# Sixteen small scalings on ScalarE, a second queue for turned inverses, and an earlier residual

## The reference

```python
q, k, v = causal_dwconv(x @ Wq.T), causal_dwconv(x @ Wk.T), causal_dwconv(x @ Wv.T)   # 4 taps and a bias each
g, beta = log_sigmoid(x @ Wg.T), sigmoid(x @ Wb.T)
k = k / clip(norm(k), 1e-12); q = q * 64 ** -0.5
for t in range(T):                 # S: 64x64 per sequence and head
    S = exp(g[t]) * S + beta[t] * (outer(v[t], k[t]) - outer(S k[t], k[t]))
    o[t] = S q[t]
x = layernorm(x + o @ Wo.T)        # then the experts, and layernorm again
```

## Time and profile before

| | |
|---|---|
| median of 3 runs | 1891.66 us (1887.62 to 1893.59) |
| profiled execution | 1890.86 us, span 1888.9 us |
| busy over the span | TensorE 1621.4, VectorE 1302.2, ScalarE 669.4, GpSimd 1068.5 us |
| 203 to 1160 us (957 us) | TensorE 909.0, VectorE 889.8, ScalarE 426.9, GpSimd 557.3 us; granted clock 1.00 |
| 64 to 203 us (139 us) | TensorE 114.3, VectorE 109.3, ScalarE 57.8, GpSimd 65.0 us; granted clock 0.93 |
| 1160 to 1276 us (116 us) | TensorE 89.6, VectorE 63.9, ScalarE 32.3, GpSimd 38.1 us; granted clock 0.92 |
| line 847, 64 operations | 91.3 us, mean 1427 ns |
| line 853, 64 operations | 67.6 us, mean 1056 ns |
| line 851, 64 operations | 132.3 us, mean 2067 ns |

### The profile page before, as it was taken

The page is one execution under the profiler, slowest core; times in us unless marked ns, Lnnn a source line. Parts: engine busy times, 40 slices in busy tenths (PEclk is TensorE's granted clock), DMA queues, the critical chain, the costliest instruction groups (busy, mean ns, idle before and its releaser), DMA issues. The chain is left out here.

```text
span 1888.9 us, 72945 instructions
## 1 busy us (share of the span) xinstructions
PE 1621.4 (86%) x31244; PEld 1239.6 (66%) x31244; DVE 1302.2 (69%) x3029; ACT 669.4 (35%) x1290; POOL 1068.5 (57%) x1261
## 2 busy tenths in 40 slices
PE   7479999999999999999999999776999995798950
PEld 6236666666666666666666666665888885787840
DVE  1388999999999999999899999623555553222214
ACT  1244444444444444444444444211111211233313
POOL 0155565565565565655556556412777776577853
PEclk9799999999999999999999999988999998899985
DMA  6245555555555546555545545425554551699557
GB/s 264 84 83 108 109 110 119 120 111 117 123 107 122 121 102 122 113 109 115 122 109 110 118 111 106 89 53 178 165 172 148 173 149 52 186 252 224 95 93 234
DMA packets 530210, 245.39 MB, mean 130 GB/s; under 512 B 423504, under 2 KB 497872, under 8 KB 528992
## 3 DMA queue, kind: packets, MB, share of 16 engines
q1 hardware_dynamic: 443872, 204.95, 43.5%
q0 software_dynamic: 18432, 18.99, 5.8%
q10 hardware_dynamic: 67584, 16.79, 4.0%
HBM read 169.29 MB, written 71.37 MB: 127 GB/s over the span
## 5 line engine op out<-in xcount | busy, mean ns | idle before, releaser
L373 PE MATMUL delta_p_j<-delta_xt,delta_w 128*128 128x512 f32 x768 | 389.2, 630 | 30.0 <-DMA delta_xt<-in_xt 17.4
L572 DVE SCALAR_TENSOR_TENSOR delta_kq<-delta_hist,cw,delta_kq 128x512 f32<-128x512 f32 x384 | 367.6, 957 | 32.6 <-ACT delta_kq L718 23.6
L711 ACT ACTIVATE delta_hist<-delta_p_j 128x512 f32<-128x512 f32 x192 | 114.9, 599 | 473.2 <-PE delta_p_j L373 464.9
L373 PEld LDWEIGHTS delta_p_j<-delta_xt,delta_w 128*128 128x128 f32 x768 | 132.5, 192 | 145.8 <-issue 112.3
L1220 POOL DMA_INDIRECT slot_tokens<-mix_tokens,mix_slot x192 | 189.9, 989 | 62.4 <-issue 61.8
L860 POOL TENSOR_TENSOR delta_sd<-state,eg_end 128x256 f32<-128x256 f32 x128 | 104.9, 820 | 203.1 <-DVE state L652 203.1
L586 DVE SCALAR_TENSOR_TENSOR delta_yv<-delta_hist,cw,delta_yv 128x512 f32<-128x512 f32 x128 | 166.3, 1299 | 7.5 <-ACT delta_yv L718 5.3
L434 PEld LDWEIGHTS delta_p_i<-delta_kkq,rt 64*64 64x64 f32 x4096 | 130.5, 135 | 59.1 <-issue 44.0
L492 PEld LDWEIGHTS delta_p_c<-delta_r,delta_kkq 64*64 64x64 f32 x2048 | 70.9, 136 | 125.1 <-DVE delta_r L644 71.3
L1343 DVE SCALAR_TENSOR_TENSOR expert_gate<-expert_gate,expert_p_h 88x256 f32<-88x256 f32 x64 | 26.7, 417 | 176.9 <-ACT expert_gate L1363 176.9
L434 PE MATMUL delta_p_i<-delta_kkq,rt 64*64 64x32 f32 (+1 forms) x4096 | 141.6, 213 | 4.5 <-DVE delta_kkq L636 3.8
(11 more groups left out here) (145 smaller groups left out, 3699.5 us busy)
## 6 DMA issues: line engine op xcount, KB each, us to landing
delta_xd<-x_scratch SPq DMA_DIRECT2D x256, 128.0 KB, 4.4
delta_w<-in_wqkv SPq DMA_DIRECT2D x64, 416.0 KB
w<-in_w SPq DMA_DIRECT2D x64, 352.0 KB
delta_eg<-eg_rows SPq DMA_DIRECT2D x128, 130.0 KB
n_scratch<-delta_kkq ACTq DMA_DIRECT2D x128, 128.0 KB
mix_ot<-ot SPq DMA_DIRECT2D x16, 1024.0 KB, 5.7
w<-in_w SPq DMA_DIRECT2D x64, 176.0 KB
ot<-delta_o SPq DMA_DIRECT2D x32, 256.0 KB
```

What stands on the lines that cost most here:

```text
L373: mm = pe.matmul(p_j[:, :], w[e][:, (ch * 3 + n) * 128:(ch * 3 + n) * 128 + 128], xt[m // 8 % 2][:, ch * 512:ch * 512 + 512], start=ch == ...
L572: ve.scalar_tensor_tensor(out, view(hist[e], i * 2 * 518 + tap, (259, 2), (1, 256)), cw[:, column:column + 1], out, ALU.mult, ALU.add).the ...
L711: ac.activation(view(hist[e], n * 518 + 3, (259, 2), (1, 256)), p_j[:, :], ACT.Copy)
```

## The change

- The two scalings move from GpSimd to ScalarE, as 8 activations of 128x64 each with the factor as a per-partition scale. `scale_keys(t-1)` stands at the end of ScalarE's slot, `scale_values(t-2)` in two groups of four, before the exponential and after `turned_r`. GpSimd keeps the power (`roots`), and waits in `factors` and `roots` until the scalings of the macro before are done.
- The turned inverses are stored by ScalarE on its DMA queue, right after it has turned them, under their own semaphore. `load_inverse` waits for them first and issues the two loads of the turned half under a semaphore of their own, then waits for the plain store and issues the other two.
- VectorE's second residual stands behind the first of the three key taps.
- GpSimd does the first decay and the off-diagonal mask before carry in.

```diff
             def load_inverse(m):
-                sp.wait_ge(x_out[group % 2], 32 * (group // 2 + 1))
+                sp.wait_ge(xt_out[group % 2], 16 * (group // 2 + 1))
                 for sh in range(2):
...
+                    sp.dma_start(view(xd[e], 512, (C, 8), (1, C), parts=half(sh)),
...
+                                         [[C, C], [UNIT, 8], [1, C]])).then_inc(xdt_in[e], 16)
+                sp.wait_ge(x_out[group % 2], 16 * (group // 2 + 1))
+                for sh in range(2):
+                    sp.dma_start(view(xd[e], 0, (C, 8), (1, C), parts=half(sh)),
...
             def inverse_r(m):
-                pe.wait_ge(xd_in[m % 2], 64 * (m // 2 + 1))
+                pe.wait_ge(xdt_in[m % 2], 32 * (m // 2 + 1))
             def inverse_rx(m):
                 pe.wait_ge(rt_out, m + 1)
+                pe.wait_ge(xd_in[m % 2], 32 * (m // 2 + 1))
...
                 if is_macro(m):
-                    conv(m, 0, tap_k, conv_k)
+                    conv(m, 0, tap_k, conv_k, (2,))
+                if two_:
+                    residual(*two_)
+                if is_macro(m):
+                    conv(m, 0, tap_k, conv_k, (1, 0))
...
-                if two_:
-                    residual(*two_)
...
             def turned_r(m):
                 ac.activation(view(rt, 0, (C, 8), (1, 48)), view(p_i, 0, (C, 8), (1, 48)), ACT.Copy).then_inc(rt_out, 1)
+                ac.wait_ge(xd_in[m % 2], 32 * (m // 2 + 1))
...
+            def store_turned(group):
+                if group >= 2:
+                    ac.wait_ge(xdt_in[0], 32 * (group - 1))
+                    ac.wait_ge(xdt_in[1], 32 * (group - 1))
+                ac.wait_ge(xit_out, group + 1)
+                ac.dma_start(bass.AP(s.x_scratch[group % 2], REGION, [[LANE, 128], [C, SUB], [1, SUB]]),
+                             view(xit, 0, (SUB, SUB), (1, SUB))).then_inc(xt_out[group % 2], 16)
+
+            def scale_keys(m):
+                ac.wait_ge(clipped_bp, 2 * m + 2)
+                ac.wait_ge(kv_out, m + 1)
+                for g in range(8):
+                    at = ring(m) + g * C
+                    ac.activation(kpv[:, at:at + C], kpv[:, at:at + C], ACT.Copy, scale=fk[:, g:g + 1]).then_inc(kp_out, 1)
+
+            def scale_values(m, units):
+                ac.wait_ge(small, m + 1)
+                for g in units:
+                    at = ring(m) + 512 + g * C
+                    ac.activation(kpv[:, at:at + C], kpv[:, at:at + C], ACT.Copy, scale=root[:, g:g + 1]).then_inc(vp_out, 1)
...
             def factors(m):
                 po.wait_ge(recip, m + 1)
+                if m >= 1:
+                    po.wait_ge(kp_out, 8 * m)
...
-            def scale_keys(m):
-                po.tensor_tensor(view(kpv, ring(m), (C, 8), (1, C)), view(kpv, ring(m), (C, 8), (1, C)),
-                                 view(fk, 0, (1, 8), (0, C)), ALU.mult).then_inc(kp_out, 1)
-            def scale_values(m):
+            def roots(m):
+                if m >= 1:
+                    po.wait_ge(vp_out, 8 * m)
                 po.tensor_tensor(root[:, :], n2[:, :], view(s.half_power, 0, (0, 8)), ALU.pow).then_inc(small, 1)
-                po.wait_ge(small, m + 1)
-                po.tensor_tensor(view(kpv, ring(m) + 512, (C, 8), (1, C)), view(kpv, ring(m) + 512, (C, 8), (1, C)),
-                                 view(root, 0, (1, 8), (0, C)), ALU.mult).then_inc(vp_out, 1)
```

More of the change, by code:

```diff
@@ L220, in delta_phase @@
         xt_in, w_in, r_in, eg_in, kk_out = both("xt_in"), both("w_in"), both("r_in"), both("eg_in"), both("kk_out")
-        kb_in, x_out, xd_in, o_out = sem("d_kb_in"), both("x_out"), both("xd_in"), both("o_out")
+        kb_in, x_out, xt_out, o_out = sem("d_kb_in"), both("x_out"), both("xt_out"), both("o_out")
+        xd_in, xdt_in = both("xd_in"), both("xdt_in")
         proj_k, proj_v, proj_q = sem("d_proj_k"), sem("d_proj_v"), sem("d_proj_q")
@@ L301, in store_inverse @@
                 if group >= 2:
-                    sp.wait_ge(xd_in[0], 64 * (group - 1))
-                    sp.wait_ge(xd_in[1], 64 * (group - 1))
+                    sp.wait_ge(xd_in[0], 32 * (group - 1))
+                    sp.wait_ge(xd_in[1], 32 * (group - 1))
                 sp.wait_ge(subst, 30 * (group + 1))
@@ L314, in load_inverse @@
                     sp.wait_ge(tt_out, m - 1)
-                sp.wait_ge(x_out[group % 2], 32 * (group // 2 + 1))
+                sp.wait_ge(xt_out[group % 2], 16 * (group // 2 + 1))
                 for sh in range(2):
[L317 to L320, removed]
+                    sp.dma_start(view(xd[e], 512, (C, 8), (1, C), parts=half(sh)),
+                                 bass.AP(s.x_scratch[group % 2], REGION + (e * 16 + sh * 8) * UNIT,
+                                         [[C, C], [UNIT, 8], [1, C]])).then_inc(xdt_in[e], 16)
+                sp.wait_ge(x_out[group % 2], 16 * (group // 2 + 1))
+                for sh in range(2):
+                    sp.dma_start(view(xd[e], 0, (C, 8), (1, C), parts=half(sh)),
+                                 bass.AP(s.x_scratch[group % 2], (e * 16 + sh * 8) * UNIT,
+                                         [[C, C], [UNIT, 8], [1, C]])).then_inc(xd_in[e], 16)
             def store_o(group):
@@ L500, in chain_update @@
                 if c == 0:
-                    pe.wait_ge(kp_out, group * 2 + 2)
+                    pe.wait_ge(kp_out, 8 * (group * 2 + 2))
                 for q in range(2):
@@ L560, in _, with conv @@
         def _(ve):
-            def conv(m, i, tapped, done):
+            def conv(m, i, tapped, done, taps=(2, 1, 0)):
                 e = m % 2
                 out = view(kq[e], i * 512, (256, 2), (1, 256))
-                for tap in (2, 1, 0):
+                for tap in taps:
                     if tap == 2:
@@ L642, in residual @@
                 if c == 0:
-                    ve.wait_ge(vp_out, group * 2 + 2)
+                    ve.wait_ge(vp_out, 8 * (group * 2 + 2))
                 ve.tensor_tensor(view(r, 0, (128, 2), (C, 2), (1, C)),
@@ L781, in _ @@
                     last_tap(m, 0, kq[m % 2][:, 0:512], tap_k)
+                if is_macro(t - 2):
+                    scale_values(t - 2, range(0, 4))
                 if is_macro(before):
@@ L787, in _ @@
                     turned_r(mi)
+                if is_macro(t - 2):
+                    scale_values(t - 2, range(4, 8))
                 if is_macro(m):
@@ L800, in _ @@
                     last_tap(m, 1, kq[m % 2][:, 512:1024], tap_q)
+                if is_macro(before):
+                    scale_keys(before)
         @block.gpsimd
@@ L878, in _ @@
                     if group >= 1:
-                        po.wait_ge(x_out[(group - 1) % 2], 32 * ((group - 1) // 2 + 1))
+                        po.wait_ge(x_out[(group - 1) % 2], 16 * ((group - 1) // 2 + 1))
+                        po.wait_ge(xit_out, group)
                     po.tensor_copy(xi[:, :], const[:, C_EYE:C_EYE + SUB * SUB]).then_inc(xi_set, 1)
@@ L886, in _ @@
                     weight(before)
-                    scale_keys(before)
-                    scale_values(before)
+                    roots(before)
 def expert_weights(sp, a, s, e):
```

15 lines of the change are left out of this document (5 added, 10 removed).

## The result

| | before | after | forecast |
|---|---|---|---|
| median of the runs, us | 1889.6 (1886.9 to 1893.6, 4) | 1836.5 (1834.9 to 1838.3, 4) | 1838 |
| profiled execution, us | 1890.9, span 1888.9 | 1834.9, span 1833.0 | 1838 |
| slot period, us | 18.015 | 17.17 | 17.11 |

Time after over time before is 0.972, with a 95% interval of 0.969 to 0.974. The time of the forecast's own case came out. The terms behind it came out less evenly, partly by errors that cancel, and the experiments show that the time belongs to no single part.

The account below looks back on a forecast made before the run. TensorE and VectorE were nearly full; TensorE's 1.31 us of waiting per 18.015 us slot was all to win. (18.015 - 17.11) x 53 = 48 us plus 5 at the edges gave 53, so 1838 us, range 1811 to 1877.

Parts of the forecast that it names:

- case A: TensorE's last inverse product becomes the bound: 0.41 us new wait per slot, period 17.11, 1838 us; the forecast itself, chance 0.45.
- 70 us of waiting: TensorE over 53 steady slots: 1.31 us of waiting per slot, all that the change can win there.
- Part 1: Scalings leave GpSimd: VectorE's query taps save 1.06 us and second value tap 0.66, 1.7 us less per slot.
- rival D: GpSimd's power operation holds VectorE's second value tap until it ends, 1.5 us: period 18.6, 1917 us; chance 0.07.
- Part 2: Sixteen scalings per slot on ScalarE at 0.26 us each fit into its free time and cost nothing.
- Rival C: ScalarE becomes late, scalings 0.36 us apart: period about 17.5, 1859 us, or about 1875 at 0.50 apart; chance 0.23.
- Part 3: Turned inverses loaded first: 1.5 us less issue, TensorE's 12.6 us wait gone, 2 us off each of first and last group.
- Part 4: Second residual forward on VectorE: TensorE's residual and state waits go, but the last inverse product waits 0.41 us per slot.
- Rival E: No change, as the residual's early place costs VectorE what it gives: period near 18.0, 1886 to 1896 us; chance 0.07.
- The floor: TensorE's slot period without any wait, summed from stretches of its own order with no wait shown: 16.70 us.
- rival B: The 0.41 us wait before the last inverse product is not there: period 16.70, 1816 us; chance 0.18.
- Edges: Outside the steady slots: 4 us for the inverses and 1 us for slots 7 and 8.

Follow-up runs that it names:

- S and T: Changed kernel with the second residual back behind all three key taps and the substitution rows, scalings and turned inverses still changed: 1833.9 us, ratio 0.970.
- the middle place: Changed kernel with the second residual behind all three key taps, ahead of the substitution rows: 1828.8 us, ratio 0.969; run again, 1827.4 us, 0.964.
- S and R: Changed kernel with the turned inverses' stores, semaphore and loads as before, scalings and residual still moved: 1896.8 us, ratio 1.005.
- S alone: Kernel before with only the scalings moved to ScalarE and GpSimd's new order: 1866.6 us, ratio 0.989.
- R alone: Kernel before with only the second residual moved forward: 1920.6 us, ratio 1.017.
- its second run: Changed kernel run again with no further edit, beside other kernels on one chip: 1844.1 us, ratio 0.973.

## Why the prediction was right, step by step

**The chain to the last inverse product (case A).** The place was right, the size of the wait was not. The stretch is 8.95 us against 9.02; TensorE's wait is 0.20 on the mean of the 47 listed, 0.17 in the slot shown, against 0.41. That the period is nevertheless 17.17 against 17.11 is in part luck: the forecast was 16.70 without waits and 0.41 of waiting, the fifty slots have 16.96 busy and 0.25 idle, two errors that cancel to within 0.1. Before the change they have 17.10 and 0.91, where the prediction read 16.70 and 1.31; its 70 us of waiting stand against 46 us in the list of TensorE's waits. That this chain decides is shown by the kernels in which it is longer: 0.66 us more of value taps goes with 0.62 more of wait, 0.89 with 0.83.

**Part 1, taps without GpSimd beside them.** Right in size: 1.65 us per slot against 1.7. The query taps shown take 2.37 us, where 2.35 was forecast. The second value tap has a median of 0.751 us inside, where it had 1.412 before; the first, 1.355, is as it was (1.354). Of the two value taps shown, together 2.14, the first still lies on line 877 (642.86 to 643.90), and the second lies inside the power operation:

```profile
642.86 1.04 POOL L877 TENSOR_TENSOR ex<-ex,delta_bp 128x512 f32<-128x512 f32 x1
643.86 2.11 POOL L883 TENSOR_TENSOR delta_root<-delta_n,half_power 128x8 f32<-128x8 f32 x1
```

```profile
L589 DVE SCALAR_TENSOR_TENSOR delta_yv<-delta_hist,cw,delta_yv x2: 750/1054/1357, 643.1 to 644.5; 128x512 f32<-128x512 f32 x2
```

The second tap took 0.750 us from 644.5 on, in the middle of the 2.11 us; the first, beside the 512-column multiplication, 1.357. So rival D is out. The Trainium skill (SBUF — State Buffer, "Who interferes with whom") calls the ports that VectorE and GpSimd share an exclusive lock, has an operation with two SBUF inputs contend for it, and says of VectorE's two-port modes that the later operation is blocked for the whole of the earlier one; the prediction put these together. The measurement decides against that for this operation on 8 columns. For the 512-column one the section's direction holds: the tap that began 0.2 us into a GpSimd operation of 1.04 us took 0.61 longer.

**Part 2, ScalarE.** The price was right, the room was not. Timeline of ScalarE:

```profile
627.65 2.01 ACT L773 ACTIVATE delta_kpv<-delta_kpv,delta_fk 128x64 f32<-128x64 f32 x8
629.75 1.33 ACTq L795 DMA_DIRECT2D n_scratch<-delta_kkq  x2
632.14 0.60 ACT L716 ACTIVATE delta_hist<-delta_p_j 128x512 f32<-128x512 f32 x1 [2.48 <-PE delta_p_j L375]
...
645.64 1.30 ACT L773 ACTIVATE delta_kpv<-delta_kpv,delta_fk 128x64 f32<-128x64 f32 x5
646.78 0.60 ACTq L795 DMA_DIRECT2D n_scratch<-delta_kkq  x1
646.84 0.81 ACT L773 ACTIVATE delta_kpv<-delta_kpv,delta_fk 128x64 f32<-128x64 f32 x3
...
649.18 0.60 ACT L716 ACTIVATE delta_hist<-delta_p_j 128x512 f32<-128x512 f32 x1 [1.53 <-PE delta_p_j L375]
```

Eight scalings take 2.01 us, (2.01 - 0.34) / 7 = 0.24 apart, against 0.26. The prediction's estimate of 239 ns from the figures of the Trainium skill (ScalarE: Activation LUTs, "What ACT_TABLE_LOAD costs") agrees. "It just fits" was wrong: after scalings and stores 1.53 and 2.48 us are idle in the two slots shown. The working put operations and DMA issues end to end; the trace has the issue at 646.78 beside scalings that run until 647.65. Rival C, at 0.23, had too much weight; eight more scalings did not produce it.

**Part 3, turned inverses.** The mechanism was right, the size was off in what it protects. The prediction counted a wait of 12.6 us and took it away. With the scalings moved but the loads as they were, that wait becomes 21.4, and with the residual moved too 32.5 us and 13 us of lowered clock. Taken from the finished kernel, the part is worth 60 us, and alone it gives 8 to 10.

**Part 4, the residual forward.** The step that failed, behind a total that held: it was credited with removing the residual's and the state's waits. The chain of 9.02 us and the idle of VectorE that it named are both there: 2.2 us on the mean in odd slots, where 1.8 was forecast, and 0.7 in even ones. But S and T without the move reach the same time, the move alone costs 1.7%, and the middle place gives 5 to 17 us more than the early one. Rival E's reason, that the early place costs as much as it gives, was true; its time was not, since Part 1 held. The prediction never worked out the move against its own absence with Part 1 in place: VectorE, 1.65 us lighter, is then late for the residual by only 13.8 / 30 = 0.46, in even slots.

**The floor.** 16.70 us was put together from stretches with no wait shown. The middle place removes nearly all waits for other engines and still has 16.95. Half of what is left in its list, 7.6 of 15.2 us, is "issue", as here in the changed kernel:

```profile
617.80 0.61 PE L436 MATMUL delta_p_i<-delta_xd,noff 64*64 64x48 f32 x15
619.23 0.61 PE L436 MATMUL delta_p_i<-delta_xd,noff 64*64 64x48 f32 x15 [0.82 <-issue]
```

TensorE stops in the middle of 32 products that wait for nothing. A sum of undisturbed stretches leaves such stops out; rival B's 1816 us was below what any version reached. The stops are some 0.14 us per slot, half of the 0.25 by which 16.95 lies over 16.70. Their cause was not tested.

**Edges.** The steady slots gave 53 x 0.845 = 45 us where 48 were forecast, and the edges 55.9 - 45 = 11 where 5 were: two errors that partly cancel in the total. Between 60 and 203 us the wait of 3.8 us for the inverses is gone; behind 1160 us 11.4 us became 4.0.

## What to carry to other kernels

Before a change in several parts is judged, work out each part against its absence in the finished kernel, not in the old one: two waits of TensorE in series hide each other, and a part that gives 10 us alone can be worth 60 behind the others. An operation on one engine that no one waits for can still be on the critical path, through the operations of another engine that it slows down. And an instruction that must wait for another engine belongs where that wait has just ended: here a place two taps too early made VectorE stand still in every slot, and all that came behind it was late.

## What was not expected of the hardware

- At or behind some waits TensorE's granted clock fell from 1.00 to 0.5 for 3.4 us (twice for 6.8), at otherwise full load. Between 203 and 1160 us this came 7 times in the kernel with S and R, each time at or right behind a wait of 1.4 to 2.8 us for a load, twice with S alone, once each with R alone and in the kernel before, never in the changed one. Where it came, the wait cost 1.7 us more than its length. Which waits do it stays open: four of 1.4 to 1.8 us in the same kernel were not followed by a fall, and with the two idle multiplications on GpSimd it came 7 times behind waits of 1.1 to 1.4 us for VectorE.
- TensorE stops in the middle of a run of matmuls for 0.3 to 1.1 us with no releaser shown, 7 times between 203 and 1160 us in the changed kernel, 10 times in its second run and 12 times with the middle place. The traces do not show what it waits for.
